# Both attentions of a transformer and graph block rebuilt: K and V spread by transfers, work in three pieces

## The reference, cut to what matters

```
cmod = silu(c) @ w_ada + b_ada                 # six (32,128) tables: shifts, scales, gates
xm   = ln(x) * (1 + scale_msa) + shift_msa
k, q, v = split(xm @ w_qkv)                    # 16 heads of 8 channels, 32 keys
x1   = x + gate_msa * (softmax(q.k / 8) v @ w_proj + b_proj)
x2   = x1 + gate_mlp * (gelu(xm2 @ w_mlp1 + b_mlp1) @ w_mlp2 + b_mlp2)     # xm2 from ln(x1)

self = [x2, c or 0 where rowsum(x2) == 0] @ W_self.T + b_self
out  = self
for d in 0, 1:                                 # d = 1: the edges transposed
    A    = edge labels (32, 32, 20 keys, 11 labels)
    bias = A @ w_bias + b_bias;  penalty -9e15 where no label is set
    w    = softmax(q_d . k_d / sqrt(8) + bias + penalty)      # 16 heads, 20 keys
    out += (w self[:20]) @ Wout_d + bout_d
result = x2 + relu(out)
```

## Time and profile before

| | us |
|---|---|
| median of 3 runs (lowest, highest) | 123.54 (122.87, 125.81) |
| span of the profiled execution | 123.5 |
| TensorE busy, of the span | 92.0 |
| VectorE busy | 75.9 |
| GpSimd busy | 60.4 |
| ScalarE busy | 51.8 |

### The profile page before, as it was taken

One profiled execution on the slowest core, in us unless ns is written; L12 is line 12 of the kernel. 1 busy time (PEld: TensorE's weight loads), 2 busy tenths in 40 slices (PEclk: granted clock), 3 DMA queues, 4 the chain that ended last, 5 costly groups with the idle time before them and its releaser, 6 DMA issues.

```text
span 123.5 us, 5275 instructions
## 1 busy us (share of the span) xinstructions
PE 92.0 (75%) x2278; PEld 56.0 (45%) x2278; DVE 75.9 (61%) x206; ACT 51.8 (42%) x91; POOL 60.4 (49%) x94
## 2 busy tenths in 40 slices
PE   0170889979649547978968997899999596869960
PEld 0170454646524335431513336435668354648740
DVE  5879669978606887124579114327948147745893
ACT  3100166568035410825000567864354297543530
POOL 7598029999700099800110434842297943244700
PEclk9999999999986995599999999999999999995996
DMA  2999100000000000000000000000000000000023
GB/s 63 395 441 425 45 5 0 8 0 5 5 5 3 0 0 5 0 5 0 0 0 0 3 0 5 5 0 5 0 5 5 8 0 5 5 5 0 5 62 113
DMA packets 2246, 5.08 MB, mean 41 GB/s; under 512 B 304, under 2 KB 1456, under 8 KB 1968
## 3 DMA queue, kind: packets, MB, share of 16 engines
q1 hardware_dynamic: 1792, 3.70, 7.7%
q10 hardware_dynamic: 432, 1.05, 2.3%
HBM read 4.23 MB, written 0.52 MB: 38 GB/s over the span
## 4 chain that ended last, share of the span: by engine, by line
PE 63%; DVE 18%; issue 10%; DMA 4%; POOL 2%; ACT 1%; SPq 0%; DVEq 0%
PE ps_t L581 9%; PE ps_y L595 8%; PE ps_s L569 7%; PE ps_d L513 7%; PE ps_d L454 5%; PE ps_d L484 5%; DVE xn_tok L694 5%; DMA w_ada_sb<-in_w_ada 4%; PE ps_d L544 4%; PE ps_d L536 3%; PE ps_d L518 3%; PE ps_d L491 3%; PE ps_d L504 2%; DVE gated L762 2%; PE ps_d L524 2%
## 5 line engine op out<-in xcount | busy, mean ns | idle before, releaser
L671 ACT ACTIVATE PT<-ps_t 128x512 f32<-128x512 f32 x24 | 14.3, 597 | 22.4 <-PE ps_t L581 22.3
L428 POOL TENSOR_TENSOR E<-E,neg_max 128x320 f32<-128x320 f32 x16 | 11.6, 726 | 21.0 <-DVE neg_max L854 20.2
L373 POOL TENSOR_TENSOR rstd<-var_eps,minus_half 128x4 f32<-128x4 f32 (+1 forms) x5 | 4.5, 897 | 26.5 <-DVE var_eps L690 26.5
L581 PE MATMUL ps_t<-ident,E 128*128 128x128 f32 x96 | 16.5, 299 | 0.8 <-issue 0.8
L846 DVE TENSOR_TENSOR E<-ps_s,bias_dir 128x320 f32<-128x320 f32 x16 | 7.8, 490 | 13.2 <-PE ps_s L569 13.0
L595 PEld LDWEIGHTS ps_y<-Vz,PT 128*32 128x32 f32 x768 | 9.7, 118 | 11.4 <-issue 7.2
L595 PE MATMUL ps_y<-Vz,PT 128*32 128x36 f32 x768 | 12.7, 210 | 2.9 <-DVE y_tok L885 1.3
L581 PEld LDWEIGHTS ps_t<-ident,E 128*128 128x128 f32 x96 | 11.5, 151 | 5.9 <-issue 5.0
L435 POOL TENSOR_SCALAR Kb<-k_raw,cols,head_mask 128x320 f32<-128x320 f32 x16 | 9.6, 613 | 7.9 <-ACT k_raw L647 7.9
L877 DVE RECIPROCAL rden<-ps_y 128x16 f32<-128x16 f32 x24 | 6.1, 254 | 11.0 <-PE ps_y L595 10.9
L634 ACT ACTIVATE hidden<-ps_d,cols 128x512 f32<-128x512 f32 x8 | 5.5, 687 | 13.6 <-PE ps_d L513 13.6
(11 more groups left out here) (95 smaller groups left out, 167.8 us busy)
## 6 DMA issues: line engine op xcount, KB each, us to landing
tok<-in_adj SPq DMA_DIRECT2D x1, 1408.0 KB, 8.9
w_rest_sb<-in_w_rest SPq DMA_DIRECT2D x1, 1088.0 KB, 11.0
x_tok<-in_x_tok ACTq DMA_DIRECT2D x2, 256.0 KB, 4.2
xT<-in_xT ACTq DMA_DIRECT2D x1, 512.0 KB, 7.8
w_ada_sb<-in_w_ada SPq DMA_DIRECT2D x1, 384.0 KB, 4.6
out<-x_tok SPq DMA_DIRECT2D x1, 256.0 KB, 3.1
w_qkv_sb<-in_w_qkv SPq DMA_DIRECT2D x1, 192.0 KB, 5.4
out<-x_tok SPq DMA_DIRECT2D x1, 192.0 KB, 2.1
```

Source lines behind the costliest of these rows:

```text
L428: pool.tensor_tensor(e, e, neg_max[:, i % 3, :].unsqueeze(2).broadcast_to([P, H, M]), ALU.add)\
L581: ins = pe.transpose(ps_t[:, j * P:(j + 1) * P], E[:, i % 3, j * HI:(j + 1) * HI, :], ident[:, :])
L671: act.activation(PT[:, i % 2, :, :], ps_t[:, :].rearrange("p (j t) -> p j t", t=P), ACT.Exp)\
```

## The change

- Layer 0 comes in five chunks (1, 1, 2, 2, 2 groups, `CHUNKS`), everything later in three pieces (3, 3, 2 groups, `MIDS`), in a new `ORDER`. Graph units alternate directions.
- K: one copy from PSUM to `k0_raw` or `k1_raw`, then four transfers from SBUF to SBUF on SP (`spread`), each with every fourth row, into a `Kb0` or `Kb1` that POOL has cleared; the weights' columns are permuted on the host to fit. Chunk 0 alone is still masked by four ACT copies. The POOL `keys` stage is gone.
- V: one copy to `v0_raw` or `v1_raw` on VectorE, which carry their column of ones, then four transfers (layer 0) or eight (graph). 18 spreads in all, 84 transfers.
- Graph units hold six heads of 20 keys in 120 rows: three turns and three products per batch for `values` (54, 54, 36 columns) where there were four (36 each).
- Label sums: the labels come transposed (352 rows in three blocks), ACT converts them to float (`adjf`), TensorE sums them with a selector matrix (`sel`, made by POOL) in 24 products of 256 columns, VectorE makes penalty and bias. POOL's 11-label loop is gone.
- The two dense banks, `ps_t` and `ps_y` become four banks `ps_b` for all uses. `PT` has three buffers in place of two.
- `recip` and `mult` take pairs of units (`PAIRS`, 13 for 24).
- `sub` of the graph layer moves from POOL to VectorE; `shift`, `resid1`, `resid2` and the sum of the directions move from VectorE to POOL (`ya`, `yb`), copies of q to ACT. All clears are POOL's; the first, of Kb0, stands ahead of `ident`.
- 24 transposes of ident run on TensorE before its first product (`WARM`). Silu is one ACT function. Layer 0's `apply` is a scalar_tensor_tensor. The labels are loaded last on SP. Stores go in five parts.

```diff
+SIX = 6
+CH = 3
+CW = C + 1
+UW = H * CW
+KR = SIX * M
+EW = CH * KR
...
+CHUNKS = [(0, 1), (1, 2), (2, 4), (4, 6), (6, 8)]
+MIDS = [(0, 3), (3, 6), (6, 8)]
+PAIRS = [(0, 1), (2,), (3, 4), (5,), (6, 7), (8, 9), (10, 11), (12, 13), (14, 15), (16, 17), (18, 19), (20, 21), (22, 23)]
+XLOADS = [(0, 1), (1, 4), (4, 8)]
+K_MASKED = {0}
+WARM = 24
...
+ORDER = [('zero', 'kb0'), ('fetch', 0), ('gbias', 0), ('fetch', 1), ('plus1', 0), ('ident', 0), ('fetch', 2),
+ ('stats', (0, 0)), ('zero', 'v0_ones'), ('consts', 0), ('zero', 'vz0a'), ('silu', 0), ('stats', (0, 2)),
+ ('dense', ('cmod', 1)), ('stats', (0, 1)), ('dense', ('cmod', 0)), ('adjf', 0), ('take', (('cmod', 1), 0)),
+ ('take', (('cmod', 0), 0)), ('stats', (0, 3)), ('rstd', (0, 1)), ('rstd', (0, 0)), ('adjf', 1), ('apply', 1),
+ ('rstd', (0, 2)), ('masks', 0), ('dense', ('xnT', 1)), ('adjf', 2), ('apply', 0), ('rstd', (0, 3)),
...
+ ('take', (('v', 2), 0)), ('spread', ('k', 2)), ('dense', ('bias', 0)), ('max', 0), ('sub', 0),
+ ('dense', ('xnT', 4)), ('shift', (0, 3)), ('dense', ('q', 2)), ('spread', ('v', 1)), ('take', (('xnT', 4), 0)),
+ ('scores', 1), ('zero', 'vz1b'), ('take', (('q', 2), 0)), ('dense', ('k', 3)), ('max', 1), ('dense', ('q', 3)),
+ ('take', (('k', 3), 0)), ('dense', ('bias', 1)), ('sub', 1), ('take', (('q', 3), 0)), ('spread', ('k', 3)),
+ ('scores', 2), ('pen', 0), ('turn', 1), ('max', 2), ('turn', 0), ('spread', ('v', 0)), ('shift', (0, 4)),
+ ('dense', ('v', 3)), ('bdir', 0), ('sub', 2), ('zero', 'vz1a'), ('dense', ('k', 4)), ('take', (('v', 3), 0)),
+ ('exp', 1), ('scores', 3), ('bturn', 0), ('spread', ('v', 2)), ('dense', ('q', 4)), ('exp', 0), ('max', 3),
+ ('turn', 2), ('take', (('k', 4), 0)), ('dense', ('v', 4)), ('take', (('q', 4), 0)), ('sub', 3), ('exp', 2),
+ ('take', (('v', 4), 0)), ('spread', ('v', 3)), ('scores', 4), ('values', 0), ('turn', 3), ('max', 4),
...
+ ('spread', ('k1', 2, 1)), ('turn', 16), ('max', 18), ('scores', 19), ('take', (('v1', 2, 0), 0)),
+ ('dense', ('q1', 2, 0)), ('exp', 16), ('badd', 19), ('values', 16), ('take', (('q1', 2, 0), 0)), ('turn', 17),
+ ('sub', 18), ('spread', ('v1', 2)), ('max', 19), ('scores', 20), ('exp', 17), ('turn', 18), ('mult', 8),
+ ('values', 17), ('badd', 20), ('exp', 18), ('ya', 3), ('recip', 9), ('values', 18), ('yb', 3), ('sub', 19),
+ ('scores', 21), ('max', 20), ('turn', 19), ('badd', 21), ('exp', 19), ('sub', 20), ('scores', 22), ('max', 21),
+ ('values', 19), ('turn', 20), ('badd', 22), ('sub', 21), ('exp', 20), ('scores', 23), ('max', 22), ('turn', 21),
+ ('badd', 23), ('exp', 21), ('values', 20), ('sub', 22), ('max', 23), ('values', 21), ('turn', 22), ('mult', 9),
+ ('sub', 23), ('ya', 4), ('exp', 22), ('recip', 11), ('turn', 23), ('yb', 4), ('recip', 10), ('values', 22),
+ ('mult', 11), ('exp', 23), ('mult', 10), ('ya', 6), ('relu', 4), ('values', 23), ('relu', 2), ('ya', 5),
+ ('relu', 3), ('store', (2, 3)), ('recip', 12), ('yb', 6), ('mult', 12), ('yb', 5), ('relu', 6), ('ya', 7),
+ ('relu', 5), ('store', (6, 7)), ('yb', 7), ('store', (3, 6)), ('relu', 7), ('store', (7, 8))]
...
+        Kb0 = sb("Kb0", [P, HI, B, S])
+        v0_raw = sb("v0_raw", [P, B, HJ, CW])
+        Vz0 = sb("Vz0", [P, HI, B, HJ, CW])
+        k1_raw = sb("k1_raw", [P, 2, DIRS, UB12, M])
+        Kb1 = sb("Kb1", [P, 2, DIRS, HI, UB12, M])
+        v1_raw = sb("v1_raw", [P, 2, HJ, UB12, DIRS, CW])
+        Vz1 = sb("Vz1", [P, 2, SIX, CH, UB12, DIRS, CW])
         E0 = sb("E0", [P, 3, H, S])
-        E1 = sb("E1", [P, 3, H, S])
-        PT = sb("PT", [P, 2, HJ, P])
-        neg_max = sb("neg_max", [P, 3, H])
-        rden = sb("rden", [P, 2, HJ, HI])
+        E1 = sb("E1", [P, 3, EW])
+        PT = sb("PT", [P, 3, HJ, P])
...
+                elif stage == "spread" and key[0] == "k":
+                    g0, g1, bs = batches("k", key[1])
+                    for s in fresh("sp", ("take", (key, 0)), ("zero", "kb0")):
+                        sp.wait_ge(*s)
+                    for i in range(HI):
+                        sp.dma_start(Kb0[i:P:HI, i, bs, :], k0_raw[i:P:HI, bs, :]).then_inc(spread_done[key], 16)
...
+                    for i in range(SIX):
+                        to = slice(M * i, M * i + M)
+                        for c in range(1 if i < HI else 2):
+                            quad, j, c1 = (i, 0, CH) if i < HI else ((i - HI) * 2 + c, CH, c + 1)
+                            of = slice(QUAD * quad, QUAD * quad + M)
+                            sp.dma_start(Vz1[to, k, i, c:c1, 0:nb, :, :].rearrange("p c b d w -> p c (b d w)"),
+                                         v1_raw[of, k, j:j + c1 - c, 0:nb, :, :].rearrange("p c b d w -> p c (b d w)"))\
+                              .then_inc(spread_done[key], 16)
...
+                    for c in range(3):
+                        rows = ADJ_ROWS[c][1] - ADJ_ROWS[c][0]
+                        for s in fresh("pe", ("adjf", c)):
+                            pe.wait_ge(*s)
+                        for b in range(UB):
+                            t = adj_f[0:rows, c, :].rearrange("p (g b q) -> p g b q", b=UB, q=S)[:, :, b, :]
+                            ins = pe.matmul(ps[QUAD * b:QUAD * b + QUAD, which * G * S:(which + 1) * G * S],
+                                            sel[0:rows, which, c, :], t, start=(c == 0), stop=(c == 2))
+                    return ins
...
+            for i in range(WARM):
+                pe.transpose(ps_s[:, i % HJ, 0:P], ident[:, :], ident[:, :])
...
+                            heads = min(SIX, H - c * SIX)
+                            rows, w = heads * M, heads * CW
+                            for b in range(UB):
+                                V = Vz1[0:rows, slot_of(m), 0:heads, c, (g - MIDS[m][0]) * UB + b, d, :]
+                                ins = pe.matmul(ps[QUAD * b:QUAD * b + QUAD, o + c * SIX * CW:o + c * SIX * CW + w],
+                                                PT[0:rows, key % 3, c, b * S:(b + 1) * S], V, start=True, stop=True)
...
+                elif stage == "adjf":
+                    for s in fresh("act", ("load", f"adj{key}")):
+                        act.wait_ge(*s)
+                    rows = ADJ_ROWS[key][1] - ADJ_ROWS[key][0]
+                    ins = act.activation(adj_f[0:rows, key, :], adj_i[0:rows, key, :], ACT.Copy)
...
+                    return dve.tensor_copy(v0_raw[:, bs, :, 0:C].rearrange("p b j c -> p (b j) c"),
+                                           ps[:, 0:nb * S].rearrange("p (r c) -> p r c", c=C))
...
+                    for g in range(*CHUNKS[key]):
+                        ins = dve.scalar_tensor_tensor(out=xn_tok[:, g, :], in0=x_tok[:, g, :],
+                                                       scalar=meanvar[:, g, 0:1],
+                                                       in1=rstd[:, 0, g:g + 1].broadcast_to([P, P]),
+                                                       op0=ALU.subtract, op1=ALU.mult)
```

More of the change, by code:

```diff
@@ new lines @@
+CHUNKS = [(0, 1), (1, 2), (2, 4), (4, 6), (6, 8)]
[4 more added lines that the diff above has]
+WARM = 24
+ON = {'adjf': 'act',
+ 'consts': 'pool',
+ 'dense': 'pe',
+ 'exp': 'act',
+ 'fetch': 'sp',
+ 'ident': 'pool',
+ 'resid1': 'pool',
+ 'resid2': 'pool',
+ 'rstd': 'pool',
+ 'scores': 'pe',
+ 'sel': 'pool',
+ 'selfb': 'pool',
+ 'shift': 'pool',
+ 'silu': 'act',
+ 'spread': 'sp',
+ 'store': 'sp',
+ 'sub': 'dve',
+ 'turn': 'pe',
+ 'values': 'pe',
+ 'ya': 'pool',
+ 'yb': 'pool',
+ 'zero': 'pool',
+ ('shift', (0, 0)): 'dve'}
@@ new lines, in units_of_mid, with v1_parts, parts_of, freed_by @@
+def units_of_mid(m):
+    return [n for n in L1_UNITS if MIDS[m][0] <= UNITS[n][2] < MIDS[m][1]]
+def v1_parts(m):
+    g0, g1 = MIDS[m]
+    return [(g, min(g + 2, g1)) for g in range(g0, g1, 2)]
+def parts_of(name):
+    kind = kind_of(name)
+    if kind == "k" and name[1] in K_MASKED:
+        return range(HI)
+    return range(1)
+def freed_by(user):
+    kind = kind_of(user)
+    if kind == "turn":
+        return [("exp", user[1])]
+    if kind == "values":
+        return [("mult", user[1])]
+    if kind == "bias":
+        return [("pen", 0), ("bdir", 0)]
+    if kind == "x1tok":
+        return [("stats", (1, user[1])), ("take", (user, 0))]
+    return [("take", (user, part)) for part in parts_of(user)]
@@ L202, in program, with bank_user @@
+def bank_user(stage, key):
+    if stage == "dense":
+        return ("bias", 0) if kind_of(key) == "bias" else key
+    if stage == "turn":
+        return ("turn", key)
+    if stage == "values":
+        return ("values", pair_of(key))
+    return None
 def program(nc, cols, x_tok, xT, adj, w_ada, w_qkv, w_rest, out):
@@ new lines, in shift, with resid @@
+        def shift(engine, name, layer, p):
+            g0, g1 = norm_chunk(layer, p)
+            bs = slice(g0 * UB, g1 * UB)
+            for s in fresh(name, ("take", (("xn2T" if layer else "xnT", p), 0))):
+                engine.wait_ge(*s)
```

(11 more changed lines are left out.)

1453 lines of the change are left out of this document (840 added, 613 removed), and 15 rows, old and new, of tables (BANKS, ORDER, UNITS).

## The result

| | before | after |
|---|---|---|
| median of 4 runs, us (lowest, highest) | 124.42 (122.87, 125.81) | 118.92 (118.08, 120.71) |
| span of the profiled execution | 123.5 | 116.2 |
| TensorE / VectorE busy | 92.0 / 75.9 | 93.4 / 72.0 |
| GpSimd / ScalarE busy | 60.4 / 51.8 | 44.5 / 43.2 |

The ratio is 0.959 (95% interval 0.949 to 0.969): some 5 us faster where 9.8 were forecast. 118.92 lies inside the range and 5.2 us over the forecast of 113.7.

What follows compares the result with a forecast made beforehand. TensorE bounds the kernel, its work hardly changing, so gains must come from its losses: work 78.2 + start 14.5 + middle 8.0 + graph part 8.5 + tail 4.5 = 113.7 us; range 104 to 123, own range 110 to 118.

Steps and rivals of the forecast that it cites:

- Time outside the span: Whole kernel: the profiled span, 123.5 us, was taken as the median of the runs, with nothing added.
- SP's queue: Layer-0 spreads: 36 issues at 0.43, 15.5 us of SP; last issued by 31, in by 33, covered by TensorE work.
- the graph part: From 66.3 to the last values: TensorE loses 8.5 us, where it lost 8.3, with other contents.
- The rival of the transfers: Before first scores or values and at layer-0 chunks: TensorE waits for spreads, 14 us more, 127.7 in all; chance 0.13.
- VectorE in the last stretch: From scores 16 on: VectorE needs 21 us against TensorE's 14.5, costing TensorE 6.5, of which 1.5 counts in the tail.
- thirds don't fill: Rival for the middle's norm chains: they stay as long, the middle keeps 16.1 less 1, 120.7 us; chance 0.15.
- Work: TensorE's tasks at their quick prices: 77.5 us before, 78.2 after the change, so hardly different.
- The start: Up to 21 us: first k product near 14.3, loss 14.5 us, 0.9 less than before, bounds of 3 either way.
- the quick price: Time of each TensorE task in the chain's well-fed stretches, such as 1.02 us for 64 records of V.
- ACT is the other late one: At the start: ACT converts three label blocks ahead of its first k take; last load landed at 13.6 us.
- The middle and the tail: Middle, 21 to 66: loss 8.0 us for 16.1. Tail, after the last values: 4.5 for 6.2.
- the forecast's cuts: Windows of the old kernel, cut at 21.0, 66.3 and 117.3 us: first turn, start of graph work, last values.

Runs made afterwards that it cites:

- the second profile of the changed kernel: The changed kernel run again with no edit: median 119.44 us, one run disturbed at 160.07, no ratio given; profiled span 114.4.
- The version with both K maskings and the shorter start: Changed kernel with both K maskings, no clear ahead of ident, no warming turns, third label conversion behind first q copies: 113.73 us, 0.911; again 112.67, 0.918.
- The two further edits: On both K maskings and shorter start: subtractions of units 18 to 23 on GpSimd, 112.50 us; then also residuals and two shifts on VectorE, 112.72.
- the last four runs: Both K maskings with shorter start, 113.73 us; again, 112.67; plus subtractions of units 18 to 23 on GpSimd, 112.50; plus residuals and two shifts on VectorE, 112.72.

## Why the prediction was right and wrong

**Time outside the span.** The prediction took the span of 123.5 for the time of the runs "so nothing is added for the difference". Every run with both numbers has 1.7 to 2.1 us between them: 118.08 against 116.2, and 123.61 against 121.7 for the kernel before. In spans, 113.7 was forecast and 116.2 measured, so 2.5 of the 5.2 us are the kernel's and 1.9 are this step; the rest is the difference between the profiled execution and the median.

**The step that failed: SP's queue.** "36 issues, 15.5 us of SP from about 15.5 on, so the last (v 4) is issued by 31 and in by 33." The start was near (16.83) and so was the landing of 2.0 (values 0 began 2.2 behind v 0's last issue). The term that was mis-sized is the price of an issue: 0.60 and 0.04 of gap where I had 0.43, and five of 36 at 1.0 to 1.4. The issues took 25.8 us, 10.3 more than forecast; 1.55 of waiting for ScalarE's copy came on top. I had taken the price from loads, the only rows of before.

That time counts because the queue is in order. Values 0 need the fifth spread, which had landed by 34.6, where I had 26. In the graph part I had set one eight-part V spread, 5.4 us, against 9 us of TensorE work, and not against the eight K issues in front of it: the last piece's 16 issues are 12.8 us from 94.61, and the values of its four units stand behind all of them. Of the 3.9 us that TensorE idled from 94.6 to 108.7, 3.15 are waits for these spreads (2.35 and 0.80). Four runs carry this: 11.5 us more queue cost 9 us, 16 issues fewer gave 3.5, 8 fewer at the end 2.4, and both together 5.0.

**The rival of the transfers** had the place right (K and V spreads, later spreads behind one on SP) and its deciding point wrong: it was to decide if a landing took over 4 us, while landings stayed near 2 and the issue decided. Its 14 us were too many: PE's own waits for spreads come to 7.8 us in the rows above.

**The second step that failed: VectorE in the last stretch.** It was to cost TensorE 6.5 us. It was busy for 10.74 of 14.08 us there, and moving six subtractions off it changed nothing even with the queue relieved (112.50 and 112.67). Its own operations cost as forecast, here those that answer to the earlier trace rows:

```profile
L560 DVE TENSOR_TENSOR E<-E,neg_max 128x320 f32<-128x320 f32 x16 | 8.0, 498 | 0.1
...
L1217 DVE TENSOR_REDUCE neg_max<-E 128x16 f32<-128x320 f32 x16 | 7.4, 468 | 0.1
```

So the prices were right, but I summed 19 us of it "from scores 16 on" as if it all had to stand behind them; in the trace VectorE finished most of each unit in the time in which TensorE waited or did the last piece's products. The forecast had 5.0 us for VectorE (6.5 less 1.5) that the runs don't show, and nothing for the queue, whose two cut places were worth 5.0. That the total is nearer than the steps is luck. It is luck, too, that 118.9 lies near the 120.7 of the rival "thirds don't fill": the thirds did fill, from 61 on.

**Work.** TensorE's busy time rose by 1.4 (92.0 to 93.4), where I had 0.7 more work. The two don't compare as they stand: 5.4 of the 93.4 are the 24 warming turns, so that what is left, 88.0, is 4.0 less than before. Label sums took 1.51 + 1.50 = 3.0 for 2.6: quarters do run beside each other. Three turns took 0.33 to 0.49 in the chain (0.44 forecast), values 0.40 for most units as before, so that the 0.6 us saved there weren't found.

**The start.** ident at 4.57 (4.5), cmod 9.79 to 11.66 (9.6 to 11.2), the first apply from 12.71 to 13.05 (13.0): right. The old 3.97 us operations are gone, as this line shows against the earlier trace rows. Two things changed at once, the operation and GpSimd's clears, none of which ran beside it, and no run separates them:

```profile
12.71 0.34 DVE L1178 SCALAR_TENSOR_TENSOR xn_tok<-x_tok,meanvar,rstd 128x128 f32<-128x128 f32 x1
```

Behind it I lost: the first k product came at 15.6 (14.3), the first scores at 21.2 (18). TensorE waited 1.5 for the apply at the end of cmod, and its work from 15.27 to 21.2, without a gap, cost more than the same work did later: the granted clock was at 0.50, the lower level, from 15.74 to 21, although the 24 turns had kept TensorE busy until 10.0. But a granted clock of 1.00 would not have saved that time. Here are 64 records of V in the changed kernel, whose window stands in the table above with 0.50, then the same window and records in the run without the turns:

```profile
17.84 1.08 PE L773 MATMUL ps_b<-w_qkv_sb,xm 128*32 128x32 f32 x64
```

```profile
15.74:21.00 5.26, 3.67 (x76) 2.74 (x78) 1.37 (x5) 3.12 (x10) 1.45 (x2) 1.00 0.06 15
...
18.48 1.08 PE L773 MATMUL ps_b<-w_qkv_sb,xm 128*32 128x32 f32 x64
```

The row of the window has a clock of 1.00 (before the last two columns), and the price is the same 1.08. The kernel before paid 1.08 at 16.4 as well, with 1.00 in its row. Later the same records take 0.76. So at the start a granted clock of 1.00 doesn't give the quick price, and what does isn't shown. "ACT is the other late one" was right, and I gave it no price; the run without warming turns shows it at 3.29. In the second profile of the changed kernel the chain begins with the labels' load (10% of the span) and two conversions, and not with the turns.

**The middle and the tail.** Thirds filled the norm chains from 61 on, better than forecast. From 21 to 61 TensorE idled 7.4 us, of which 4.7 are waits for spreads, and the granted clock fell to 0.5 twice (slices 13 and 17 of the page), where I expected 1.0. In the second profile of the same kernel, with waits of the same kind up to 1.7 us, it didn't fall there. From the end of the last values, 111.9, to the end are 4.3 us for the 4.5 forecast.

By the forecast's cuts, with the same quick prices: work 79.2 (78.2: 0.4 more for the label sums, 0.6 for the values), tail 4.3 (4.5), start about 15.5 (14.5; an estimate, 2.6 us of quick work in the 5.26 of that stretch and some 2.9 before it), and for middle and graph part 17.2 is left of 116.2, for 16.5 forecast. The sum by stretches is thus near in spans; inside the last two of them the contents were others than forecast.

## What to carry to other kernels

When compute instructions are traded for transfers, price the queue that issues them as an engine: so many issues by the duration of the same kind of transfer (from SBUF to SBUF if it is that), in their order, from the first to the one that the next stage needs; only then add the landing. The same masks were cheaper here as four ScalarE copies in layer 0 (0.931 against 0.959), and in the last graph piece besides (0.919), so a mix of both, by which engine has room in that stretch, beat transfers throughout; masks throughout weren't run. And put an engine's work of a stretch against its deadline there only after checking what of it can be done before the stretch begins.

The version with both K maskings and the shorter start took 113.7 and 112.7 in two rounds, 0.911 and 0.918 of before, against 118.9 and 0.959 for the changed kernel. The two further edits added nothing to it.

## What the hardware showed that I had not expected

- The issue of a small transfer took SP 0.43 us from device memory to SBUF, 0.60 from SBUF to SBUF, and 0.71 to 0.89 with one more dimension, whether 32 or 128 partitions took part in the first two. In each long row of issues some took 1.0 to 1.8. The landings, 1.7 to 3.5 us behind the issue with most near 2, were the part of the price that mattered less. The Trainium skill (DMA: Bandwidth & Descriptors, Anatomy of one DMA) puts the fixed cost of a transfer issued by GpSimd at about 2 us; these were issued by SyncE, and their landings agree with that figure.
- Issued from ScalarE, most of the same transfers took 0.51 to 0.85 us of that engine's own order of work each, and the kernel 14 us.
- The warming turns went together with a low granted clock, not a high one. All eight profiled executions with the 24 turns show it at 0.5 in slice 6, which lies between 13.9 and 19.5 us; the five without the turns show 0.9 or more there, among them the run in which the turns were the only edit. What ties the one to the other stays open. The slices of the run with both K maskings and the turns, and then of the same with the start shortened:

```profile
PEclk9999755599999999999999999999999999999985
```

```profile
PEclk9999999999999999999999999999999999999997
```

- In the profiles of the last four runs, all without the turns and with the short queue, the granted clock was 0.98 to 0.99 over the span; 0.90 in the changed kernel, 0.94 with the short queue and the turns, 0.95 without the turns and with the long queue. The times show no gain from the higher clock at the start: 0.972 without the turns and 0.959 with them, 0.911 and 0.918 with the shortened start and 0.919 without.
- Between the span of an execution and its time lay 1.7 to 2.1 us in each.
